# Two-block feed-forward network with 2:4 sparse hidden values on one core: the low part moved to VectorE, and the second down product issued in one piece

## The chip, the core and the metric

The kernel runs on one core of a Trainium2 chip. The metric is the time on the device in microseconds (us); the time before is the median of three runs. The engines are TensorE (PE, with its weight loads as PEld), VectorE (DVE), ScalarE (ACT), GpSimd (POOL) and SyncE (SP), which issues the DMAs.

## The reference

One sequence of 2048 tokens with 256 features passes through six residual parts. The parts are: a feed-forward part with ternary weights, an attention with ALiBi, the same feed-forward part again, a feed-forward part with 2:4 sparse hidden values, an attention with rotary positions, and the sparse part again. Only the sparse part is touched:

```python
def _sparsify_2to4(h):
    g = h.reshape(B, S, I // 4, 4)
    a = jnp.abs(g)
    _, idx = jax.lax.top_k(a, 2)
    mask = (pos == idx[..., 0:1]) | (pos == idx[..., 1:2])
    return (g * mask.astype(g.dtype)).reshape(B, S, I)
h = jax.nn.silu(x @ w_gate) * (x @ w_up)      # x: 2048 x 256, h: 2048 x 1024
return _sparsify_2to4(h) @ w_down             # used as x + 0.5 * f(layernorm(x))
...
```

Of each group of four hidden values the two with the largest magnitude are kept.

## The kernel before

All phases run one after the other on the core. The sparse part is the function ffn_phase with ternary set to false; it runs twice, as ffn1a and as ffn1b. In the profiled execution ffn1a begins at about 860 us and ffn1b at about 1622 us and runs to the end of the kernel.

A phase works through NB = 4 blocks of BLK = 512 tokens. Block 0 and block 3 are written out, blocks 1 and 2 are a hardware loop (blocks_of). The hidden size of 1024 is cut into NCH = 8 chunks of 128, in two halves of GCH = 4 chunks; the host has sorted the weights so that the four members of a sparse group lie in the four chunks of one half at the same place. To keep f32 accuracy each operand of TensorE is a high part plus a low part, and each product is three matmuls (high by high, high by low, low by high).

Each engine has its own program, in order, and semaphores tie them together. For a chunk c of block b:

- TensorE, gate_up(b, c), L361: 12 matmuls of 512 columns into two PSUM banks.
- ScalarE, silu, L431; VectorE, multiply, L485, gives h; ScalarE, side, L451, writes the magnitudes of h into the tile abs.
- VectorE, choose(b, u, i): the 2:4 choice for half u, in four steps. Steps 0 and 1 compare pairs of magnitudes (three operations each, tile win, L502); step 2 adds up ranks (L506 to L509); step 3 finishes them (L512 to L515) and writes the kept values over abs (four operations, L519, semaphore keep).
- ScalarE, hi, L438: the kept values rounded to the high part hh. GpSimd, lo, L580: kept value minus hh gives the low part hl, one 128x512 operation for each chunk, 32 in a phase. A helper lo with the same operation stands in VectorE's program too, but before the change only the ternary phases call it (L490).
- TensorE, down(b, u), L372: 48 matmuls of 256 columns for half u. It waits for all four low parts of the half (semaphore hlo). VectorE, residual, L532, adds the result to the resident x once semaphore dn says that both halves are done.
- For the next block: VectorE's dve_stats at c = 1 and dve_normalise (tile xn, L124) at c = 5, TensorE's transposes(b + 1) (L143) between chunks 6 and 7, ScalarE's act_hi (tile xh, L151) and VectorE's dve_lo (tile xl, L158) at the start of c = 7. Chunk 0 of the next block waits for xl.

The work lags. In the body of block b, VectorE makes the choice of the first half of block b in chunks 4 to 7 and that of the second half of block b - 1 in chunks 0 to 3. TensorE issues down(b - 1, 0) behind chunk 4. It issues down(b - 1, 1) in two pieces: tiles 0 and 1 behind chunk 6, ahead of the transposes, and tiles 2 and 3 behind chunk 7. In block 3 that product is in one piece behind chunk 7. After the last block the rest is drained: choice of the last half, low parts, down(3, 0), down(3, 1), residual. GpSimd does the first four low parts of block b - 1 at the start of its body, then the small power operation rstd for the next layer norm (L136), then the other four.

Of the kernel before, what the change touches and what calls it, by code (L numbers as in the profile page):

```python
# [21 lines left out]
F32 = mybir.dt.float32  # L22
F32R = mybir.dt.float32r
BF16 = mybir.dt.bfloat16
ALU = mybir.AluOpType
# [8 lines left out]
NB = TOK // BLK  # L34
TPB = BLK // P
# [4 lines left out]
NCH = HID // P  # L40
GCH = 4
# [47 lines left out]
def is_first(b):  # L89
    return isinstance(b, int) and b == 0  # L90


def is_last(b):
    return isinstance(b, int) and b == NB - 1
# [204 lines left out]
def ffn_phase(nc, g, name, ternary, out=None, ahead=()):  # L299
# [12 lines left out]
    with ExitStack() as ctx:  # L312
# [32 lines left out]
        @block.tensor  # L345
        def _(e):
            def gate_up(b, c):
                n = b * NCH + c

                if ternary:  # L350
                    if not (is_first(b) and c < 2):
                        e.wait_ge(s.mul, n - 1)
                elif not (is_first(b) and c < 3) and c != 1:
                    e.wait_ge(s.mul, n - 1 if c in (0, NCH - 1) else n - 2)
                for half in range(2):
                    col = half * HID + c * P
                    for k in range(KD):
                        if c == 0 and half == 0:
                            e.wait_ge(s.xlo, b * KD + k + 1)
                        for q, (w, x) in enumerate(terms):  # L360
                            ins = e.matmul(g.ps[:, slots[c] + half, :], w_up[w][:, k, col:col + P], xp[x][:, k, :],  # L361
                                           start=k == 0 and q == 0, stop=k == KD - 1 and q == len(terms) - 1)
                ins.then_inc(s.gu, 1)

            def down(b, u, tiles=range(TPB)):
                e.wait_ge(s.hlo, b * NCH + u * GCH + GCH)
                if u == 0 and not is_first(b):
                    e.wait_ge(s.res, b)
                for j in tiles:
                    todo = [(i, w, x) for i in range(GCH) for w, x in terms]  # L370
                    for q, (i, w, x) in enumerate(todo):
                        ins = e.matmul(g.ps[:, 6 + j // 2, (j % 2) * D:(j % 2 + 1) * D], hp[x][:, u, i, j * P:(j + 1) * P],  # L372
                                       w_dn[w][:, u * GCH + i, :], start=u == 0 and q == 0 and j % 2 == 0,
                                       stop=u == 1 and q == len(todo) - 1, skip_group_check=True)
                if j == TPB - 1:
                    ins.then_inc(s.dn if u else s.dnh, 1)

            def squares(b):

                e.wait_ge(s.sqc, b * NCH + NCH)  # L380
                for j in range(TPB):
                    for u in range(2):
                        ins = e.matmul(g.ps[:, 4, j:j + 1], ssq[:, u, j * P:(j + 1) * P], g.one_col[:, :],
                                       start=j == 0 and u == 0, stop=u == 1, skip_group_check=True)
                ins.then_inc(s.sqs, 1)

            def transposes(b):
                e.wait_ge(s.xn, b + 1)
                if not is_first(b):
                    if ternary and not (isinstance(b, int) and b == 1):  # L390
                        e.wait_ge(s.ms, b - 1)
                    if not ternary:
                        e.wait_ge(s.mul, b * NCH - 3)
                pe_transpose(e, g, s, b, lambda j, k: g.xn[:, j, k * P:(k + 1) * P], TB)

            def body(b):
                for c in range(NCH):
                    gate_up(b, c)
                    if ternary:
                        if c == 2 and not is_first(b):  # L400
                            squares(b - 1)
                            down(b - 1, 1)
                        if c == NCH - 1:
                            down(b, 0)
                    elif not is_first(b):
                        if c == 4:
                            down(b - 1, 0)
                        if c == NCH - 2 and not is_last(b):
                            down(b - 1, 1, range(TPB // 2))
                        if c == NCH - 1:  # L410
                            down(b - 1, 1, range(0 if is_last(b) else TPB // 2, TPB))
                    if c == NCH - 2 and not is_last(b):
                        transposes(b + 1)

            transposes(0)
            blocks_of(e, body)
            if ternary:
                squares(NB - 1)
            else:
                down(NB - 1, 0)  # L420
            down(NB - 1, 1)
# [57 lines left out]
        def _(e):  # L479
# [7 lines left out]

            def lo(b, c):
                e.wait_ge(s.hhi, b * NCH + c + 1)
                e.tensor_tensor(hl[:, c // GCH, c % GCH, :], h32[:, c // GCH, c % GCH, :],  # L490
                                hh[:, c // GCH, c % GCH, :].bitcast(F32), ALU.subtract).then_inc(s.hlo, 1)

            PAIRS = [(0, 1), (0, 2), (0, 3), (1, 2), (1, 3), (2, 3)]
# [32 lines left out]
            def residual(b):  # L526
                if ternary:
                    e.wait_ge(s.inv, b + 1)
                e.wait_ge(s.dn, b + 1)
                for j in range(TPB):  # L530
                    xt = g.x[:, ds(b * TPB + j, 1), :].rearrange("p a d -> p (a d)")
                    ins = e.scalar_tensor_tensor(out=xt, in0=g.ps[:, 6 + j // 2, (j % 2) * D:(j % 2 + 1) * D],  # L532
                                                 scalar=inv[:, j:j + 1] if ternary else 0.5, in1=xt, op0=ALU.mult, op1=ALU.add)
                ins.then_inc(s.res, 1)

            def body(b):
                for c in range(NCH):
                    if c == NCH - 1 and not is_last(b):
                        dve_lo(e, g, s, b + 1, TB)
                    multiply(b, c)  # L540
                    if ternary:
                        if c:
                            lo(b, c - 1)
                        elif not is_first(b):
                            lo(b - 1, NCH - 1)
                        if c == 3 and not is_first(b):
                            mean_squares(b - 1)
                        if c == 6 and not is_first(b):
                            residual(b - 1)
                    elif c >= GCH:  # L550
                        choose(b, 0, c - GCH)
                    elif not is_first(b):
                        choose(b - 1, 1, c)
                    if not is_last(b) and c == 1:
                        dve_stats(e, g, s, b + 1)
                    if not is_last(b) and c == (3 if ternary else 5):
                        dve_normalise(e, g, s, b + 1)
                if not ternary and not is_first(b) and not is_last(b):
                    residual(b - 1)
# [4 lines left out]
            if ternary:  # L564
                lo(NB - 1, NCH - 1)
                mean_squares(NB - 1)
            else:
                for i in range(GCH):
                    choose(NB - 1, 1, i)
                    if i == 1:  # L570
                        residual(NB - 2)
            residual(NB - 1)
            e.wait_ge(s.res, NB)


        @block.gpsimd
        def _(e):
            def lo(b, c):
                e.wait_ge(s.hhi, b * NCH + c + 1)
                e.tensor_tensor(hl[:, c // GCH, c % GCH, :], hs[:, c // GCH, c % GCH, :],  # L580
                                hh[:, c // GCH, c % GCH, :].bitcast(F32), ALU.subtract).then_inc(s.hlo, 1)

            def sum_squares(b, u):
                for i in range(1, GCH):
                    n = b * NCH + u * GCH + i
# [11 lines left out]
                e.tensor_tensor(inv[:, :], ms[:, :], g.mhalf[:, :], ALU.pow).then_inc(s.inv, 1)  # L597

            def body(b):
                if not ternary and not is_first(b):  # L600
                    for c in range(GCH):
                        lo(b - 1, c)
                if not is_last(b):
                    pool_rstd(e, g, s, b + 1)
                if ternary:
                    sum_squares(b, 0)
                    if not is_first(b):
                        inverse(b - 1)
                    sum_squares(b, 1)
                elif not is_first(b):  # L610
                    for c in range(GCH, NCH):
                        lo(b - 1, c)

            pool_rstd(e, g, s, 0)
            blocks_of(e, body)
            if ternary:
                inverse(NB - 1)
            else:
                for i in range(NCH):
                    lo(NB - 1, i)  # L620

        if out is not None:
            @block.sync
# [957 lines left out]
```

## Time and profile before

| | us |
|---|---|
| median of 3 runs (lowest to highest) | 1806.38 (1805.32 to 1822.72) |
| profiled execution, its own time | 1802.62 |
| its span, first to last instruction | 1800.4 |
| busy over the span: PE / DVE / ACT / POOL | 1556.4 / 1283.4 / 950.9 / 306.7 |

The span is 2.2 us shorter than the profiled execution's own time. Busy times of different engines overlap, so they don't add up to the span. The time of an instruction in the timeline runs from its start to its end; one engine's neighbours overlap by about 0.08 us, so that what an instruction adds to a row of others is the distance from start to start.

### The profile page before, as it was taken

The page shows a single profiled execution, that of the slowest core. Times are in us where ns is not written, and L with a number is a line of the kernel's source. Part 1 is how long each engine was busy: PE and PEld are TensorE (multiplying, and loading weights), DVE is VectorE, ACT ScalarE, POOL GpSimd, SP SyncE. Part 2 cuts the span into 40 slices and gives each one's busy share as a digit, 9 for nine tenths or more (in the row PEclk, how much of TensorE's full clock was granted, in tenths as well). Part 3 has the DMA queues.
Part 4 walks back from the last instruction along what each step waited for, and adds up shares of the span by engine and source line. Part 5 has one row for each costly group of instructions (what it writes and reads, how often), then busy time and mean ns, then how long its engine had stood idle before and what let it go on. Part 6 is the DMA issues. An engine that isn't in the chain of part 4 may idle for free. (4 is left out here: it accounts for less than half of the span.)

```text
span 1800.4 us, 33059 instructions
## 1 busy us (share of the span) xinstructions
PE 1556.4 (86%) x13324; PEld 972.3 (54%) x13324; DVE 1283.4 (71%) x1864; ACT 950.9 (53%) x1889; POOL 306.7 (17%) x326
## 2 busy tenths in 40 slices
PE   1598878989999999887799689899999999997996
PEld 0487744444434436676588567444444444366885
DVE  8655647888898832564599786687888988025996
ACT  3345324767777784454334222456686788733342
POOL 5333100000000000232043432000000000030433
PEclk9999869999999999898899888698999999788998
DMA  5000769100000000100100058640000000020000
GB/s 201 24 1 0 127 184 129 34 14 24 13 20 7 2 2 3 46 1 24 35 1 1 1 116 199 87 69 14 20 17 16 11 2 2 2 71 1 12 12 24
DMA packets 37857, 70.54 MB, mean 39 GB/s; under 512 B 5411, under 2 KB 13219, under 8 KB 36645
## 3 DMA queue, kind: packets, MB, share of 16 engines
q1 hardware_dynamic: 37716, 68.58, 16.8%
q8 instruction: 99, 1.62, 0.4%
q14 instruction: 42, 0.34, 0.1%
HBM read 48.90 MB, written 22.15 MB: 39 GB/s over the span
## 5 line engine op out<-in xcount | busy, mean ns | idle before, releaser
L1166 DVE TENSOR_REDUCE l_att_maxima<-psum 128x2 f32<-128x1024 f32 (+3 forms) x640 | 665.0, 1063 | 135.3 <-PE psum L1064 127.6
L1258 ACT ACTIVATE l_att_probs<-psum 128x512 f32<-128x512 f32 (+3 forms) x1280 | 605.6, 531 | 250.3 <-PE psum L1092 227.8
L1109 PE MATMUL psum<-l_att_probs,l_att_v 128*17 128x256 f32 (+2 forms) x4608 | 363.5, 389 | 1.2 <-ACT l_att_o L1265 0.9
L1092 PE MATMUL psum<-l_att_qt,l_kt 51*128 51x512 f32 (+6 forms) x1280 | 331.6, 470 | 7.5 <-ACT l_att_probs L1258 7.5
L1064 PE MATMUL psum<-l_kt,l_att_qt 59*128 59x512 f32 (+7 forms) x1280 | 285.2, 422 | 5.0 <-DVE l_att_maxima L1166 2.6
L1092 PEld LDWEIGHTS psum<-l_att_qt,l_kt 59*128 59x128 f32 (+1 forms) x1280 | 142.6, 194 | 174.0 <-ACT l_att_probs L1258 161.8
L1109 PEld LDWEIGHTS psum<-l_att_probs,l_att_v 128*17 128x17 f32 x4608 | 79.5, 96 | 150.5 <-issue 101.7
L1064 PEld LDWEIGHTS psum<-l_kt,l_att_qt 59*128 59x128 f32 (+1 forms) x1280 | 139.1, 199 | 19.5 <-DVE l_att_maxima L1166 17.4
L1228 POOL CAST l_att_crow<-l_att_cneg 128x16 bf16<-128x16 f32 x32 | 8.1, 252 | 812.6 <-DVE l_att_cneg L1176 812.6
L1061 PE MATMUL psum<-tri 64*128 64x128 bf16 x1024 | 89.1, 237 | 22.0 <-DVE l_att_maxima L1166 18.8
L1090 PEld LDWEIGHTS psum<-tri 64*128 64x128 bf16 x1024 | 33.7, 96 | 101.8 <-ACT l_att_probs L1258 65.6
L1090 PE MATMUL psum<-tri 64*128 64x128 bf16 x1024 | 82.4, 228 | 1.9 <-DMA l_att_qt<-l_att_ct 1.7
L1193 DVE RECIPROCAL l_att_rinv<-psum 128x16 f32<-128x16 f32 x32 | 8.0, 250 | 106.3 <-PE psum L1128 106.3
L1061 PEld LDWEIGHTS psum<-tri 64*128 64x128 bf16 x1024 | 35.8, 101 | 59.8 <-DVE l_att_maxima L1166 34.3
L580 POOL TENSOR_TENSOR ffn1b_hl<-ffn1b_abs,ffn1b_hh 128x512 fp32r<-128x512 f32 x32 | 51.7, 1643 | 84.6 <-ACT ffn1b_hh L438 84.6
L580 POOL TENSOR_TENSOR ffn1a_hl<-ffn1a_abs,ffn1a_hh 128x512 fp32r<-128x512 f32 x32 | 51.7, 1644 | 84.6 <-ACT ffn1a_hh L438 84.6
L136 POOL TENSOR_TENSOR rstd<-var,mhalf 128x4 f32<-128x4 f32 x24 | 24.7, 1027 | 224.8 <-DVE var L115 224.8
L361 PE MATMUL psum<-ffn0b_xh,w_ternary 128*128 128x512 f32 x128 | 53.1, 415 | 9.2 <-DVE ffn0b_h L485 7.8
L361 PE MATMUL psum<-ffn0a_xh,w_ternary 128*128 128x512 f32 x128 | 52.9, 413 | 9.1 <-DVE ffn0a_h L485 7.7
L361 PE MATMUL psum<-ffn1b_xh,wgu_h 128*128 128x512 f32 x128 | 51.5, 402 | 3.9 <-DVE ffn1b_xl L158 2.8
L361 PE MATMUL psum<-ffn1a_xh,wgu_h 128*128 128x512 f32 x128 | 51.3, 400 | 3.9 <-DVE ffn1a_xl L158 2.8
L372 PE MATMUL psum<-wdn_h,ffn1b_hh 128*128 128x256 f32 x128 | 38.8, 303 | 15.6 <-DVE x_resident L532 8.9
(205 smaller groups left out, 2914.5 us busy)
## 6 DMA issues: line engine op xcount, KB each, us to landing
l_kt<-qk_scratch SPq DMA_DIRECT2D x48, 256.0 KB, 10.6
qk_scratch<-l_att_kv_parts SPq DMA_DIRECT2D x22, 512.0 KB, 7.3
l_att_qt<-qk_scratch SPq DMA_DIRECT2D x168, 64.0 KB
qk_scratch<-y SPq DMA_DIRECT2D x10, 512.0 KB, 10.7
set_raw<-in_w_gu SPq DMA_DIRECT2D x2, 1024.0 KB, 6.4
x_resident<-in_x SPq DMA_DIRECT2D x1, 2048.0 KB, 15.4
y<-in_w_gu SPq DMA_DIRECT2D x1, 2048.0 KB, 8.1
raw_down<-in_w_dn SPq DMA_DIRECT2D x2, 1024.0 KB, 8.0
```

The lines of the kernel that those rows point to most:

```text
L136: e.tensor_tensor(g.rstd[:, :], g.var[:, :], g.mhalf[:, :], ALU.pow).then_inc(s.rstd, 1)
L361: ins = e.matmul(g.ps[:, slots[c] + half, :], w_up[w][:, k, col:col + P], xp[x][:, k, :], start=k == 0 and q == 0, stop=k == KD - 1 and q ...
L372: ins = e.matmul(g.ps[:, 6 + j // 2, (j % 2) * D:(j % 2 + 1) * D], hp[x][:, u, i, j * P:(j + 1) * P], w_dn[w][:, u * GCH + i, :], start=u ...
L580: e.tensor_tensor(hl[:, c // GCH, c % GCH, :], hs[:, c // GCH, c % GCH, :], hh[:, c // GCH, c % GCH, :].bitcast(F32), ALU.subtract).then_i ...
L1061: e.matmul(g.ps[:, bank + x, w - P:w], g.tri[half, (2 + m) * P:(3 + m) * P], g.tri[half, m * P:(m + 1) * P], start=m == 0, stop=False, ski ...
L1064: e.matmul(g.ps[:, bank + x, 0:w], qt[rows_of(x), pair, t * P:(t + 1) * P], g.kt[rows_of(x), pair, c * BLK:c * BLK + w], start=c < qb, sto ...
L1090: e.matmul(g.ps[:, i % SB, off:off + P], g.tri[rows, c * P:(c + 1) * P], g.tri[rows, (2 + c) * P:(3 + c) * P], start=c == 0, stop=False, s ...
L1092: e.matmul(g.ps[:, i % SB, off:BLK], g.kt[rows_of(x), hp, kt * P:(kt + 1) * P], qt[rows_of(x), hp, off:BLK], start=u >= TPB, stop=True, sk ...
L1109: ins = e.matmul(g.ps[h * VW:h * VW + HD + 1, OB, lo:hi], g.v[:, kt, STEPS[st][1] * HG + h, :], pr[:, un % PB, h, lo:hi], start=u == 0 and ...
L1166: e.tensor_reduce(mp[:, st % 2, 2 * p:2 * p + 2, t, c], g.ps[:, bank:bank + 2, 0:w], AX.X, ALU.max).then_inc(s.mx, 1)
L1228: e.tensor_copy(cr[:, 0], whole).then_inc(s.cp, 1)
L1258: e.activation(pr[:, un % PB, h, off:BLK], g.ps[:, i % SB, off:BLK], ACT.Exp, scale=HD ** -0.5).then_inc(s.ex, 1)
```

## The change

VectorE now computes the low parts of the sparse phases, GpSimd does not any more. In the body of a block, behind the multiplication of chunk 1 come the low parts of chunks 0 and 1 of the block before, behind that of chunk 2 those of chunks 2 and 3, behind that of chunk 5 those of chunks 4 and 5, and behind that of chunk 6 those of chunks 6 and 7. At the end of the phase the first four stand behind residual(2), and the last four behind the last step of the choice. On TensorE down(b - 1, 1) is issued in one piece behind chunk 7 in every block. The ternary phases keep their instructions.

```diff
-            def down(b, u, tiles=range(TPB)):
+            def down(b, u):
...
                     elif not is_first(b):
                         if c == 4:
                             down(b - 1, 0)
-                        if c == NCH - 2 and not is_last(b):
-                            down(b - 1, 1, range(TPB // 2))
                         if c == NCH - 1:
-                            down(b - 1, 1, range(0 if is_last(b) else TPB // 2, TPB))
+                            down(b - 1, 1)
                     if c == NCH - 2 and not is_last(b):
                         transposes(b + 1)
...
             def lo(b, c):
                 e.wait_ge(s.hhi, b * NCH + c + 1)
-                e.tensor_tensor(hl[:, c // GCH, c % GCH, :], h32[:, c // GCH, c % GCH, :],
+                e.tensor_tensor(hl[:, c // GCH, c % GCH, :], hs[:, c // GCH, c % GCH, :],
...
-                    elif c >= GCH:
-                        choose(b, 0, c - GCH)
-                    elif not is_first(b):
-                        choose(b - 1, 1, c)
+                    else:
+                        if not is_first(b) and c % GCH in (1, 2):
+                            i = c // GCH * GCH + 2 * (c % GCH - 1)
+                            lo(b - 1, i)
+                            lo(b - 1, i + 1)
+                        if c >= GCH:
+                            choose(b, 0, c - GCH)
+                        elif not is_first(b):
+                            choose(b - 1, 1, c)
...
                     if i == 1:
                         residual(NB - 2)
+                        for c in range(GCH):
+                            lo(NB - 1, c)
+                for c in range(GCH, NCH):
+                    lo(NB - 1, c)
             residual(NB - 1)
...
@@ gpsimd @@
-                if not ternary and not is_first(b):
-                    for c in range(GCH):
-                        lo(b - 1, c)
                 if not is_last(b):
                     pool_rstd(e, g, s, b + 1)
...
-                elif not is_first(b):
-                    for c in range(GCH, NCH):
-                        lo(b - 1, c)
...
-            else:
-                for i in range(NCH):
-                    lo(NB - 1, i)
```

## Rows read from the trace of the kernel before

**Rows 1.** Busy time by engine in block 1 of ffn1b; then PEclk, DMA, GB/s

```profile
1663.90:1699.10 35.20, 33.13 (x190) 29.44 (x189) 32.17 (x59) 12.09 (x22) 13.44 (x9) 0.95 0.00 1
```

**Rows 2.** Timeline of PE: start, duration, work, and idle time before with its releaser

```profile
894.56 0.50 PE L361 MATMUL psum<-ffn1a_xh,wgu_h 128*128 128x512 f32 x1 [1.41 <-DVE ffn1a_xl L158]
...
970.65 0.40 PE L361 MATMUL psum<-ffn1a_xh,wgu_h 128*128 128x512 f32 x1
...
1658.37 0.50 PE L361 MATMUL psum<-ffn1b_xh,wgu_h 128*128 128x512 f32 x1 [1.41 <-DVE ffn1b_xl L158]
...
1672.14 0.28 PE L372 MATMUL psum<-wdn_h,ffn1b_hh 128*128 128x256 f32 x1
...
1685.59 0.50 PE L372 MATMUL psum<-wdn_h,ffn1b_hh 128*128 128x256 f32 x1 [2.07 <-POOL ffn1b_hl L580]
...
1727.96 0.32 PE L143 MATMUL psum<-consts,ffn1b_xn 128*128 128x128 f32 x1 [1.20 <-DVE ffn1b_xn L124]
...
1734.53 0.40 PE L361 MATMUL psum<-ffn1b_xh,wgu_h 128*128 128x512 f32 x1
...
1788.17 0.58 PE L372 MATMUL psum<-wdn_h,ffn1b_hh 128*128 128x256 f32 x1 [2.60 <-POOL ffn1b_hl L580]
```

**Rows 3.** Timeline of DVE in block 0 of ffn1b, where GpSimd has no low part

```profile
1649.88 1.89 DVE L502 TENSOR_TENSOR ffn1b_win<-ffn1b_abs 128x512 bf16<-128x512 f32 x3
...
1660.88 2.50 DVE L519 SCALAR_TENSOR_TENSOR ffn1b_abs<-ffn1b_rank,ffn1b_h 128x512 f32<-128x512 bf16 x4
```

**Rows 4.** Timeline of DVE in block 1 of ffn1b, and behind its last block

```profile
1663.30 0.68 DVE L485 TENSOR_TENSOR ffn1b_h<-ffn1b_silu,psum 128x512 f32<-128x512 f32 x1
1663.90 4.60 DVE L502 TENSOR_TENSOR ffn1b_win<-ffn1b_abs 128x512 bf16<-128x512 f32 x3
...
1669.02 2.38 DVE L502 TENSOR_TENSOR ffn1b_win<-ffn1b_abs 128x512 bf16<-128x512 f32 x3
...
1674.02 0.42 DVE L506 TENSOR_TENSOR ffn1b_rank<-ffn1b_win 128x512 bf16<-128x512 bf16 x1
...
1677.42 3.59 DVE L519 SCALAR_TENSOR_TENSOR ffn1b_abs<-ffn1b_rank,ffn1b_h 128x512 f32<-128x512 bf16 x4
...
1681.54 4.55 DVE L502 TENSOR_TENSOR ffn1b_win<-ffn1b_abs 128x512 bf16<-128x512 f32 x3
...
1688.41 1.37 DVE L124 TENSOR_SCALAR ffn1b_xn<-x_resident,mv,rstd 128x256 f32 x4
...
1739.57 0.68 DVE L485 TENSOR_TENSOR ffn1b_h<-ffn1b_silu,psum 128x512 f32<-128x512 f32 x1
...
1769.87 6.89 DVE L502 TENSOR_TENSOR ffn1b_win<-ffn1b_abs 128x512 bf16<-128x512 f32 x6
...
1780.92 3.61 DVE L519 SCALAR_TENSOR_TENSOR ffn1b_abs<-ffn1b_rank,ffn1b_h 128x512 f32<-128x512 bf16 x4
1795.68 1.42 DVE L532 SCALAR_TENSOR_TENSOR x_resident<-psum,x_resident 128x256 f32<-128x256 f32 x4 [11.15 <-PE psum L372]
```

**Rows 5.** Timeline of POOL: the low parts of half a block

```profile
1678.85 6.68 POOL L580 TENSOR_TENSOR ffn1b_hl<-ffn1b_abs,ffn1b_hh 128x512 fp32r<-128x512 f32 x4 [4.37 <-ACT ffn1b_hh L438]
```

**Rows 6.** One tile's instructions, ffn0a_hl: a low part on VectorE, min/median/max ns

```profile
L490 DVE TENSOR_TENSOR ffn0a_hl<-ffn0a_h,ffn0a_hh x32: 679/684/1768, 73.8 to 174.3; 128x512 fp32r<-128x512 f32 x32
```

**Rows 7.** Timeline of ACT at the start of block 2 of ffn1b

```profile
1699.58 0.60 ACT L431 ACTIVATE ffn1b_silu<-psum 128x512 f32<-128x512 f32 x1 [3.53 <-PE psum L361]
...
1702.68 0.59 ACT L431 ACTIVATE ffn1b_silu<-psum 128x512 f32<-128x512 f32 x1
```

**Rows 8.** Stretches behind gaps of PE, columns as in the first group

```profile
802.05:804.05 2.00, 2.00 (x6) 1.52 (x5) 0.75 (x2) 0.13 (x1) 0.00 (x0) 0.50 0.00 0
...
1686.00:1687.00 1.00, 1.00 (x7) 1.00 (x7) 1.00 (x3) 0.21 (x1) 0.00 (x0) 0.50 0.00 0
1724.00:1725.00 1.00, 1.00 (x11) 1.00 (x10) 1.00 (x3) 0.17 (x1) 0.00 (x0) 1.00 0.00 0
```

**Rows 9.** Timeline of DVE: the last residual of ffn1a

```profile
1030.37 0.76 DVE L532 SCALAR_TENSOR_TENSOR x_resident<-psum,x_resident 128x256 f32<-128x256 f32 x2 [9.72 <-PE psum L372]
```

More of the change, by code:

```diff
@@ L368, in down @@
                     e.wait_ge(s.res, b)
-                for j in tiles:
+                for j in range(TPB):
                     todo = [(i, w, x) for i in range(GCH) for w, x in terms]
@@ L374, in down @@
                                        stop=u == 1 and q == len(todo) - 1, skip_group_check=True)
-                if j == TPB - 1:
-                    ins.then_inc(s.dn if u else s.dnh, 1)
+                ins.then_inc(s.dn if u else s.dnh, 1)
             def squares(b):
@@ L577, in _ @@
         def _(e):
[L578 to L581, printed above, removed]
             def sum_squares(b, u):
```

## The prediction

> **What bounds the kernel now.** I read the groups of instructions first: everything that the diff touches lies in ffn1a and ffn1b, the rest keeps its instructions, so only these two phases can move. Then the busy time by stage, for block 1 of ffn1b: TensorE is busy 33.1 of 35.2 us and VectorE 32.2 [rows 1]. Neither is idle enough to ignore, so what matters is which waits for which. The timelines tell. From the first matmul of block 1 to that of block 3 pass 76.2 us in ffn1b and 76.1 in ffn1a, so 38.1 for a block [rows 2]. What TensorE needs without waiting is a good deal less: five products of chunks plus 0.17 us for the start take 1672.14 - 1658.37 = 13.77 us, so a chunk is 2.72 us, eight are 21.8, and 96 down matmuls of 0.12 us are 11.5; with the transposes (0.85 us to the next start) that makes 34.2 us. The missing 4 us in each block are two waits: 2.07 us for the low parts of GpSimd ahead of the first piece of down(b - 1, 1), and 1.20 us for xn ahead of the transposes, or in block 1 of ffn1b a lower clock in the place of the second [rows 2, 8]. Both are VectorE's doing in the end. It is never idle in these blocks but for some 2.8 us ahead of xl, and part of its work is stretched. Three comparisons take 1.89 us in block 0, where GpSimd has no low part to do, and 4.60 and 4.55 us in block 1 where GpSimd has; four kept values take 2.50 against 3.59 us [rows 3, 4]. GpSimd's four low parts run 6.68 us beside them [rows 5].
>
> **What the change removes.** The low parts leave GpSimd, so the stretches should go. From the first multiplication of block 1 to the end of xn, VectorE loses (4.60 - 1.89) + (2.38 - 1.89) + (3.59 - 2.50) + (4.55 - 1.89) = 7.0 us to them [rows 3, 4]. Behind the last block six comparisons take 6.89 us where 3.6 would do, and four kept values 3.61 against 2.50 [rows 4]. The 2.07 us wait for GpSimd goes as well.
>
> **What it adds on VectorE.** One low part of the same shape and types takes 0.684 us in the ternary phase, so 0.60 us from start to start [rows 6]; the upper end, 1.77 us in the same row, belongs to the overlap with GpSimd and does not come here, since GpSimd keeps only its 1 us power operation in a block. Eight a block are 4.8 us. Six of them stand ahead of xn: 3.6 us against the 7.0 saved.
>
> **What it moves on TensorE.** The first 24 matmuls of down(b - 1, 1) (2.9 us) move from ahead of the transposes to behind chunk 7. They used to fill time in which xn was not ready. Now they follow xn, in a row with everything else. The question is therefore what xn waits for.
>
> **A middle block step by step.** From start to start an operation adds some 0.08 us less than its duration: a multiplication or comparison 0.60, a rank 0.34 and four 1.34, four kept values 2.42, the normalisation 1.29, the residual 1.33; the statistics add 2.1, from the comparisons' end at 1671.3 to the multiplication ahead of 1674.02 [rows 3, 4]. Take the first matmul of the block as 0. Chunks 0 to 4 end at 2.7, 5.5, 8.2, 10.9 and 13.6. ScalarE starts silu 0.28 us behind chunk 0 and VectorE multiplies 0.63 us later, at 3.6, if it is free. Comparisons to 6.0. The second silu starts 3.1 us behind the first, since four roundings to hh stand ahead of it [rows 7], so the second multiplication starts at 6.7. Then two low parts to 8.5, comparisons to 10.3, statistics (2.1) to 12.4, multiplication to 13.0, two low parts to 14.2. down(b - 1, 0) may start at 14.3, 0.7 us late, and ends at 20.0; chunk 5 ends at 22.8. VectorE meanwhile does ranks to 15.5, multiplication 16.1, ranks 17.6, kept values 20.0, multiplication 20.6, comparisons 22.4, and then waits for chunk 5: its multiplication starts only at 23.7. Behind it stand two low parts (25.5), comparisons (27.3) and the normalisation, to 28.6. TensorE has finished chunk 6 at 25.5 and is idle for 3.2 us. Transposes to 29.6, chunk 7 to 32.4, the whole second down product to 38.2. VectorE has xl, the last choice and the residual (1.33 us) done by 40.3, ahead of the next multiplication at 38.2 + 3.6, so it delays nothing; ScalarE's magnitudes now wait for low parts a little longer, but each is done before the next silu can start. So the period is 38.2 us, against 38.1. What was saved on VectorE is spent on its own added work, on the wait for chunk 5 (which sits behind down(b - 1, 0)) and on the 2.9 us that now follow xn.
>
> **Block 1** starts with VectorE late, its first multiplication at 4.9 (1663.30 - 1658.37) [rows 2, 4], as now. By the same steps down(0, 0) starts at 15.0, xn ends at 29.2 and the block lasts 38.8 us. The two blocks together: 77.0 against 76.1, 0.9 us worse in each phase.
>
> **The last block and the drain** have no xn. VectorE's first multiplication starts at 3.6 and not at 1739.57 - 1734.53 = 5.0 [rows 2, 4]. Multiplication 5 starts at 23.0, behind chunk 5; two low parts, comparisons, multiplication, two low parts, ranks, multiplication and the choice bring VectorE to 34.2, the six comparisons to 37.8, the residual to 39.1, four low parts to 41.5. down(3, 0) runs from 41.7, at the lower clock at its start, as it does now, to 48.8. VectorE's ranks and kept values end at 46.7 and its last low part at 49.3, since the last rounding to hh must come first. So down(3, 1) starts at 49.4, right behind down(3, 0), 5.8 us at the full clock, and the last residual starts at 55.4. Now it starts at 1795.68 - 1734.53 = 61.2 in ffn1b and 1030.37 - 970.65 = 59.7 in ffn1a [rows 2, 4, 9]. That is 5.8 and 4.3 us gained; some 1.5 us of ffn1b's share is the lower clock behind the 2.60 us gap at 1788.17, which goes with the gap.
>
> Sum without the clock: 2 x 0.9 - 5.8 - 4.3 = -8.3 us.
>
> **The clock.** The new gap of some 3.2 us ahead of the transposes comes four times in the two phases. Of the eleven gaps of 2.07 to 2.60 us that the trace has in the feed-forward phases, five were followed by the lower of the two levels (0.50 is 1.2 GHz, 1.00 is 2.4 GHz), as at 1686 and 802 us, and six were not, as at 1724 us [rows 8]. One such stretch cost 1.6 us: the 24 matmuls from 1685.59 us took 4.47 us to the next start, where 24 x 0.12 = 2.88 would do [rows 2]. Everything behind the gap is in a row, so this price is paid in full. For a longer gap I take three falls in four, +4.8 us; the ends are none (0) and all four (+6.4).
>
> The Trainium skill, page "TensorE: Matmul & The Clock Gate", section "Part 1: The HAM clock gate", says that the check of activity runs free of the kernel, so that the same kernel can meet a fall in one execution and miss it in the next. By it the sum would be anything between -8.3 and -1.9 us, without a preference for three. The trace agrees in kind: two gaps of the same 2.07 us ended differently.
>
> Total: -8.3 + 4.8 = -3.5 us. The profiled execution, 1802.62 us, lies 3.8 us under the median of the runs, 1806.38. I apply the sum to the median: **1802.9 us**, 0.2% faster. A measurement of this kernel tells about 1%, 18 us, from no change.
>
> **Rivals.**
>
> *No or one fall of the clock.* The same walk, -8.3 to -6.7 us: 1798 to 1800 us. Six of eleven gaps speak for it, their being shorter against it.
>
> *TensorE never waits.* If xn were ready when chunk 6 ends, the period would be 34.2 us: four periods by 3.8 us and the drain's 10.1 give -25 us, 1781 us. For it speaks that VectorE's own work without stretches is only some 33 us a block. Against it: the multiplication behind chunk 5 and the 4.9 us between it and the end of xn lie in a row, and xn would have to come 3.1 us sooner than I find.
>
> *The stretches stay (the slower side).* If the comparisons and kept values are long for another reason than GpSimd (reads of ScalarE and writes to the same tile, say), the added 0.60 us come on top. First multiplication to end of xn is 26.5 us now [rows 4]; with 3.6 more, and 3.6 ahead and 9.6 behind it (start of transposes, 0.1; transposes and chunk 7, 3.7; down, 5.8), the period is 43.3 us, 5.3 more, four times. In the drain the last kept value, 45.0 us behind the first multiplication now [rows 4], moves by 12 x 0.6 = 7.2, and the last down product starts at about 58.3 where it is 53.6 now [rows 2]: 4.7 us, twice. Together +30 us, 1836 us, 1.7% slower. It decides from the point where less than half of the 7.0 us goes. Against it stands that none of the three comparisons or kept values of block 0 is stretched, and every stretched stretch has a low part of GpSimd beside it [rows 3 to 5].
>
> The Trainium skill, page "SBUF — State Buffer", section "SBUF: two separate sides", describes a port pair that VectorE and GpSimd hold in turn for a whole instruction, when VectorE reads two inputs from SBUF. By it the stretches end with GpSimd's low parts and this rival is worth little; the multiplications, which read one input from PSUM, keep 0.68 us beside GpSimd, which agrees [rows 4].
>
> **Chances.** Forecast (two to four falls) 0.64, no or one fall 0.25, TensorE never waits 0.04, the stretches stay 0.03, and 0.04 for runs of the whole kernel that scatter beyond 1% on either side. The walk with none to four falls gives 1798.1 to 1804.5; the drain's second product at the lower clock in both phases adds 3; a low part at its full 0.68 in place of 0.60 us adds 0.5 in each of four blocks, 2 in all; a gap shorter by 1 us in each takes 4 off. That makes 1794 to 1809. Faster by over 1%: 0.06; within 1%: 0.90; slower by over 1%: 0.04.
>
> **What would show it.** Right: comparisons of 1.89 us in all blocks; down(b - 1, 1) as 48 matmuls behind chunk 7; a gap of TensorE of about 3 us ahead of the transposes, released by xn; VectorE idle for about 1 us ahead of the multiplication of chunk 5; periods near 38 us, or 39.8 with a lower clock; no gap above 1 us ahead of the last down product. Wrong: a gap ahead of the transposes under 1 us, comparisons still above 2 us, or VectorE busy until the next block's first multiplication.

## The result and the profile after

| | us |
|---|---|
| before, 20 runs: median (lowest to highest), mean | 1804.76 (1788.81 to 1827.86), 1807.5 |
| changed, 20 runs: median (lowest to highest), mean | 1812.20 (1798.03 to 1818.45), 1810.1 |
| ratio, changed to before | 1.0051, 95% interval 1.0029 to 1.0073 |
| profiled execution of the changed kernel, its span | 1818.45, 1816.3 |

I forecast 1802.9 us, 0.2% faster, in a range of 1794 to 1809. The median came out at 1812.2, 0.5% slower by the ratio. That ratio leaves out runs that lie over 1.5% above the fastest of their own kernel; five of before (1817 to 1828 us) fall under this and none of the changed one, although the means of all runs are only 2.6 us apart. With all 20 runs of each, the ratio is 1.0014 by the means and 1.0041 by the medians, and the difference of the means, 2.6 us, has a 95% interval of 5.2 us to either side (worked out from the spread of the runs). So these two sets alone do not show that the changed kernel is slower.

So where did the time go? First the touched phases. I take each from its first transpose to its last residual. In the first trace of before ffn1a took 1030.37 - 863.28 = 167.1 us and ffn1b 1795.68 - 1626.37 = 169.3. In the changed kernel ffn1a takes 1035.46 - 867.90 = 167.6 and ffn1b 1811.60 - 1644.53 = 167.1. Together they are 1.8 us shorter, 334.6 against 336.4. The profiled execution as a whole is 15.8 us longer, so all of that and 1.8 us more lie in stages that the change does not touch: 13 us in the second attention, the rest in the stages ahead of ffn1a.

TensorE in ffn1b after the change, timeline of single instructions (start, duration, work, idle time before and its releaser); the counterparts are [rows 2]:

```profile
1676.53 0.50 PE L361 MATMUL psum<-ffn1b_xh,wgu_h 128*128 128x512 f32 x1 [1.41 <-DVE ffn1b_xl L158]
...
1706.15 0.32 PE L143 MATMUL psum<-consts,ffn1b_xn 128*128 128x128 f32 x1 [3.17 <-DVE ffn1b_xn L124]
...
1717.15 0.40 PE L361 MATMUL psum<-ffn1b_xh,wgu_h 128*128 128x512 f32 x1
...
1731.64 0.38 PE L372 MATMUL psum<-wdn_h,ffn1b_hh 128*128 128x256 f32 x1 [0.70 <-DVE ffn1b_hl L487]
...
1746.29 0.98 PE L143 MATMUL psum<-consts,ffn1b_xn 128*128 128x128 f32 x7 [3.17 <-DVE ffn1b_xn L124]
...
1755.75 0.40 PE L361 MATMUL psum<-ffn1b_xh,wgu_h 128*128 128x512 f32 x1
...
1797.42 0.58 PE L372 MATMUL psum<-wdn_h,ffn1b_hh 128*128 128x256 f32 x1 [7.14 <-DVE ffn1b_hl L487]
```

Read the brackets: the wait for GpSimd is gone, and a wait of 3.17 us for xn stands ahead of the transposes, where there was 1.20 [rows 2]. The blocks begin at 1676.53, 1717.15 and 1755.75, so they last 40.6 and 38.6 us, 79.2 together, where it was 76.2.

VectorE in block 2, from its first multiplication to xn, and the last residuals of both phases; the counterparts are [rows 3, 4, 9]:

```profile
1035.46 1.42 DVE L529 SCALAR_TENSOR_TENSOR x_resident<-psum,x_resident 128x256 f32<-128x256 f32 x4 [6.10 <-PE psum L372]
...
1720.90 0.69 DVE L482 TENSOR_TENSOR ffn1b_h<-ffn1b_silu,psum 128x512 f32<-128x512 f32 x1 [1.49 <-ACT ffn1b_silu L428]
1721.50 1.89 DVE L499 TENSOR_TENSOR ffn1b_win<-ffn1b_abs 128x512 bf16<-128x512 f32 x3
1723.98 0.69 DVE L482 TENSOR_TENSOR ffn1b_h<-ffn1b_silu,psum 128x512 f32<-128x512 f32 x1 [0.59 <-ACT ffn1b_silu L428]
1724.59 1.29 DVE L487 TENSOR_TENSOR ffn1b_hl<-ffn1b_abs,ffn1b_hh 128x512 fp32r<-128x512 f32 x2
...
1734.90 2.50 DVE L516 SCALAR_TENSOR_TENSOR ffn1b_abs<-ffn1b_rank,ffn1b_h 128x512 f32<-128x512 bf16 x4
...
1741.16 0.69 DVE L482 TENSOR_TENSOR ffn1b_h<-ffn1b_silu,psum 128x512 f32<-128x512 f32 x1 [1.35 <-ACT ffn1b_silu L428]
1741.76 1.29 DVE L487 TENSOR_TENSOR ffn1b_hl<-ffn1b_abs,ffn1b_hh 128x512 fp32r<-128x512 f32 x2
1742.97 1.89 DVE L499 TENSOR_TENSOR ffn1b_win<-ffn1b_abs 128x512 bf16<-128x512 f32 x3
1744.78 1.38 DVE L124 TENSOR_SCALAR ffn1b_xn<-x_resident,mv,rstd 128x256 f32 x4
...
1811.60 1.42 DVE L529 SCALAR_TENSOR_TENSOR x_resident<-psum,x_resident 128x256 f32<-128x256 f32 x4 [6.48 <-PE psum L372]
```

The stretches are gone: 1.89 and 2.50 us where it was 4.55 and 3.59. No single comparison of the two phases takes more than 0.69 us. The low parts cost 1.29 us for two. VectorE, which had no idle time at this place before, now waits 1.35 us ahead of the multiplication of chunk 5 (1741.16), and everything from there to xn is in a row. The multiplication came at 24.0 us of the block (1741.16 - 1717.15), the walk had 23.7; the transposes at 29.1, the walk had 28.7.

The clock behind two of the gaps, as busy time of each engine in a stretch, with PEclk third from the right:

```profile
1706.99:1708.00 1.01, 1.01 (x6) 0.87 (x5) 1.01 (x3) 0.00 (x0) 0.00 (x0) 0.65 0.00 0
...
1748.00:1749.00 1.00, 1.00 (x6) 0.82 (x5) 1.00 (x4) 0.00 (x0) 0.00 (x0) 1.00 0.00 0
```

After the same gap of 3.17 us the clock fell in block 1, 0.3 us into the first stretch (so that the mean of the stretch is 0.65), and not in block 2. In ffn1a of the same trace it fell in both blocks. That is three falls in four.

### The profile page after: what moved, and what is told of

Its sections match the earlier page's. It is cut to its first block and busy times, and to the rows that moved or that the text cites. A ratio compares the mean times of both kernels' runs of the same rounds, so it can differ in the third digit from the quotient of the medians.

```text
span 1816.3 us, 33055 instructions
## 1 busy us (share of the span) xinstructions
PE 1573.4 (87%) x13324; PEld 978.0 (54%) x13324; DVE 1271.5 (70%) x1928; ACT 951.3 (52%) x1889; POOL 203.7 (11%) x262
## 5 line engine op out<-in xcount | busy, mean ns | idle before, releaser
L1101 PE MATMUL psum<-l_att_probs,l_att_v 128*17 128x256 f32 (+2 forms) x4608 | 368.1, 393 | 1.2 <-ACT l_att_o L1257 0.9
L1084 PE MATMUL psum<-l_att_qt,l_kt 51*128 51x512 f32 (+6 forms) x1280 | 335.5, 477 | 7.5 <-ACT l_att_probs L1250 7.5
L1056 PE MATMUL psum<-l_kt,l_att_qt 59*128 59x512 f32 (+7 forms) x1280 | 290.7, 431 | 5.0 <-DVE l_att_maxima L1158 2.2
L361 PE MATMUL psum<-ffn0a_xl,w_ternary 128*128 128x512 f32 x128 | 52.4, 410 | 0.0
L361 PE MATMUL psum<-ffn0b_xl,w_ternary 128*128 128x512 f32 x128 | 52.3, 408 | 0.0
L361 PE MATMUL psum<-ffn1a_xl,wgu_h 128*128 128x512 f32 x128 | 51.5, 403 | 0.0
```

The costliest lines, as they stand in the source:

```text
L1056: e.matmul(g.ps[:, bank + x, 0:w], qt[rows_of(x), pair, t * P:(t + 1) * P], g.kt[rows_of(x), pair, c * BLK:c * BLK + w], start=c < qb, sto ...
L1084: e.matmul(g.ps[:, i % SB, off:BLK], g.kt[rows_of(x), hp, kt * P:(kt + 1) * P], qt[rows_of(x), hp, off:BLK], start=u >= TPB, stop=True, sk ...
L1101: ins = e.matmul(g.ps[h * VW:h * VW + HD + 1, OB, lo:hi], g.v[:, kt, STEPS[st][1] * HG + h, :], pr[:, un % PB, h, lo:hi], start=u == 0 and ...
```

## The experiments

**The kernels against themselves.** The first question is whether the 0.5% is the change's. I ran each kernel again, three times, with no edit.

> The kernel before, unchanged, timed against itself. Theory 1 (the touched phases moved by about -2 us as the walk had it, and the 0.5% came from scatter of TensorE's clock in stages that the change doesn't touch): ratio within 0.996 to 1.004 of 1, with single runs from 1795 to 1825 us in both; ffn1b from its first transpose to its last residual again 169 to 170 us, ffn1a 167 to 168. Rival (the change makes the untouched stages slower, by its placement in memory or by the moment at which they start): the ratio is 1 too, but the spread of single runs is too small to make 7 us between two medians of 20.

> The changed kernel again, unchanged. Theory 1: the two touched phases take 167 to 168.5 us each as in its first trace, and the ratio comes out anywhere from 0.997 to 1.005, since it hangs on the clock in the attention stages. Rival: the ratio is 1.004 to 1.006 again, and the attention stages again take some 10 us more than in the trace of the kernel before.

> The kernel before once more against itself. Theory 1 (scatter of the clock in untouched stages): mean of all runs 1804 to 1808 us, ratio 0.996 to 1.004. Rival (the 7 us between the first two medians are the change's): this kernel's mean lies 5 us or more under that of the changed kernel on the same chip.

> The changed kernel once more, beside the kernel before on the same chip. Theory 1: touched phases 167 to 168.5 us each, mean of all runs within 4 us of that of the kernel before, on either side. Rival: 5 to 9 us over it.

> The kernel before against itself, a third time. Theory 1: ratio anywhere from 0.994 to 1.004; the second attention stage, from the last residual of ffn1a to the first transpose of ffn1b, takes 589 to 609 us with a mean clock of 0.92 to 0.88. Rival (long attention stages of 604 us and more belong to kernels with the low parts on VectorE): 589 to 597 us, and mean of all runs 3 us or more under the changed kernel beside it.

> The changed kernel a third time. Theory 1: mean of all runs within 4 us of the kernel before beside it, on either side; phases 167 to 168 us. Rival: 3 to 9 us over it, attention stage 604 us or more.

The ratio of each job compares with further runs of the kernel before in that job, the reference runs. The first two of these six runs were in one job, the next two in a second and the last two in a third, each on another chip.

| run | ratio to before, 95% | mean of its 12 runs | ffn1a, ffn1b |
|---|---|---|---|
| aa_before (before itself) | 1.0035, 0.9988 to 1.0081 | 1807.7 | 167.1, 169.5 |
| after_again (changed) | 1.0042, 0.9999 to 1.0085 | 1807.5 | 167.8, 167.2 |
| aa_before2 (before itself) | 0.9942, 0.9903 to 0.9981 | 1806.1 | 169.9, 169.3 |
| after_again2 (changed) | 0.9945, 0.9903 to 0.9987 | 1804.4 | 167.9, 167.1 |
| aa_before3 (before itself) | 0.9976, 0.9927 to 1.0026 | 1805.2 | 170.1, 170.0 |
| after_again3 (changed) | 1.0004, 0.9969 to 1.0038 | 1801.6 | 167.6, 167.2 |

The kernel before differs from itself by +0.35% in one job and by -0.58% in the next, there with an interval that excludes 1 and below the 0.996 that I had expected. Beside it the changed kernel lies 0.2, 1.7 and 3.6 us lower by the mean. Over the three jobs, 36 runs each, that is 1804.5 against 1806.4 us, a difference of -1.9 us with a 95% interval of about 4.7 us to either side (worked out from the spread of the single runs, 8.3 and 11.6 us). The reference runs say the same with more scatter. The changed kernel's mean is 3.3 us over theirs in the first job and 7.5 and 5.6 us under theirs in the other two, and with them the kernel before has a mean of 1807.0 us in 116 runs (one of 1935 us, at a clock of 0.73, left out), so that the changed kernel is 2.5 us lower, with an interval of 3.3 us to either side. My 4 us to either side thus hold against the repeated runs and not against the reference runs, and single runs of the kernel before go from 1786 to 1826 us, further than I had. The ratio of after_again, 1.0042, lies in the range of theory 1 and in that of its rival and decides nothing. But the rival's 5 to 9 us slower are out, and theory 1 holds. The touched phases can be read much more finely. Both together take 334.6, 335.0, 334.9 and 334.8 us in the four traces of the changed kernel, and 336.4, 336.6, 339.2 and 340.1 in the four of before: by their means 3.2 us less.

Where does the scatter lie? I took the stage from the last residual of ffn1a to the first transpose of ffn1b, the second attention, which is the same code in both. Busy time by engine, PEclk third from the right. First the kernel before in its first trace (each line is a view of its own kernel):

```profile
1030.37:1626.37 596.00, 549.05 (x5312) 280.71 (x5313) 422.44 (x531) 351.20 (x723) 59.29 (x92) 0.90 0.23 47
```

the changed kernel in its first trace:

```profile
1035.46:1644.50 609.04, 561.89 (x5312) 284.33 (x5312) 422.44 (x531) 351.46 (x723) 59.40 (x92) 0.88 0.22 46
```

the kernel before again, in its first, second and third repeat:

```profile
1032.21:1621.20 588.99, 541.52 (x5313) 279.97 (x5313) 422.50 (x531) 350.11 (x723) 59.25 (x92) 0.92 0.23 48
```

```profile
1036.28:1645.70 609.42, 562.33 (x5312) 285.88 (x5312) 422.64 (x531) 351.52 (x723) 59.26 (x92) 0.88 0.23 46
```

```profile
1035.92:1627.20 591.28, 543.85 (x5313) 281.00 (x5313) 422.46 (x531) 350.56 (x723) 59.24 (x92) 0.91 0.23 48
```

and the changed kernel again, first and second repeat:

```profile
1038.08:1628.93 590.85, 543.92 (x5312) 281.11 (x5313) 422.40 (x531) 350.25 (x723) 59.28 (x92) 0.91 0.23 48
```

```profile
1031.85:1636.50 604.65, 558.15 (x5313) 283.44 (x5313) 422.58 (x531) 351.20 (x723) 59.28 (x92) 0.89 0.23 47
```

The second column is the length: 589 to 609 us for the same work, long where PEclk is 0.88 or 0.89 and short where it is 0.90 to 0.92. VectorE is busy 422.4 to 422.6 us in all seven. TensorE's idle time in the stage, the second column less the third, is 46.5 to 47.5 us in all seven too: only its busy time grows, from 541.5 to 562.3 us. So longer waits are not what makes the stage long. Each kernel is found at both ends, the kernel before at 589.0 and 609.4 us and the changed one at 590.9 and 609.0. So this one stage scatters by 20 us with the clock, several times what the change moved, and it does so without the change. Over all traces of this study it took over 600 us in four of the eight with the low parts on VectorE, and in one of the six with them on GpSimd (aa_before2). That is too few to say whether the long case is as frequent in both; if it were much more frequent the means above would show it, and they don't.

The record has the mean granted clock of whole executions as well, for 133 runs of the kernel before (the one of 1935 us left out) and for all 56 of the changed one. The time follows it closely (correlation -0.98): 0.01 less of the clock goes with 14 us more. With this line taken off, the changed kernel is 1.9 us shorter than the kernel before at the same clock, with a 95% interval of 0.7 us to either side. This is an estimate from a straight line through all runs. The first 20 runs of the changed kernel had a mean clock of 0.924 and its later 36 had 0.9275, which by the line is 5 of the 5.6 us between their means.

**lo_only.** Low parts on VectorE, down product in two pieces as before:

```diff
+                        if c == NCH - 2 and not is_last(b):
+                            down(b - 1, 1, range(TPB // 2))
                         if c == NCH - 1:
-                            down(b - 1, 1)
+                            down(b - 1, 1, range(0 if is_last(b) else TPB // 2, TPB))
```

> Low parts on VectorE as in the change, but down(b - 1, 1) in two pieces as before. Walk: the first piece waits for the low part of chunk 7, which stands behind the multiplication of chunk 6 on VectorE, to 30.5 us; period 39.9 us, with the lower clock behind a gap of 5 us 41.5 us, against 39.8 in the changed kernel; ffn1b about 170.5 us, ratio to before 1.001 to 1.007. Rival (issuing in one piece is what costs, since its 2.9 us follow xn): period under 38 us, ffn1b under 165 us, ratio under 0.998.

Ratio 1.0083 (1.0043 to 1.0123), ffn1a and ffn1b 172.7 and 172.6 us. TensorE's timeline, the first matmul of the first piece:

```profile
1707.30 0.58 PE L372 MATMUL psum<-wdn_h,ffn1b_hh 128*128 128x256 f32 x1 [4.88 <-DVE ffn1b_hl L490]
```

The first piece waits 4.88 us for the low part of chunk 7, as the walk had it. The blocks last 42.1 and 43.2 us where I had 41.5, the phase is 2 us longer than my number, and the ratio lies above my range. The rival falls.

**down_only.** The other half: one piece behind chunk 7, low parts still on GpSimd.

```diff
-                        if c == NCH - 2 and not is_last(b):
-                            down(b - 1, 1, range(TPB // 2))
                         if c == NCH - 1:
-                            down(b - 1, 1, range(0 if is_last(b) else TPB // 2, TPB))
+                            down(b - 1, 1)
```

> The kernel before with down(b - 1, 1) in one piece behind chunk 7, low parts still on GpSimd. Walk: VectorE stays stretched, so xn ends 26.5 us behind the first multiplication and nothing fills the wait; gap ahead of the transposes about 5 us, period 39.8 us plus 1.6 for the clock; the 2.07 us wait for GpSimd goes. ffn1b and ffn1a about 172 to 174 us each against 169.3 and 167.1, ratio 1.003 to 1.007. Rival (one piece is free or better, the wait for GpSimd was the cost): period 36 to 38 us, both phases under 168 us.

Ratio 1.0111 (1.0009 to 1.0212, four runs), both phases 177.4 us. VectorE's timeline keeps the stretched comparisons:

```profile
1688.37 4.54 DVE L499 TENSOR_TENSOR ffn1b_win<-ffn1b_abs 128x512 bf16<-128x512 f32 x3
...
1695.23 1.37 DVE L124 TENSOR_SCALAR ffn1b_xn<-x_resident,mv,rstd 128x256 f32 x4
```

and TensorE's shows the gap ahead of the transposes:

```profile
1696.74 0.47 PE L143 MATMUL psum<-consts,ffn1b_xn 128*128 128x128 f32 x1 [6.41 <-DVE ffn1b_xn L124]
```

The direction was right and the size too small, 177.4 where I had 172 to 174, and the ratio is above my range. The gap is 6.4 us in block 1 and 6.0 in block 2, not 5, and behind the second of these gaps the transposes and chunk 7 took 6.4 us in place of 3.6, so a fall of the clock can cost 2.7 us and not only 1.6. Over both phases low parts alone cost 8.9 us against the first trace of before (345.3 - 336.4), one piece alone 18.4, and both together save 1.8. The first piece can't start early when the low parts wait in VectorE's row, and xn is too late for one piece as long as VectorE is stretched, so each half pays only with the other one.

**early.** The changed kernel with xn ahead of the wait for chunk 5, and so also ahead of the multiplication, two low parts and three comparisons that stand behind that wait:

```diff
-                    if not is_last(b) and c == (3 if ternary else 5):
+                    if not is_last(b) and c == (3 if ternary else 4):
                         dve_normalise(e, g, s, b + 1)
```

> The changed kernel with the normalisation of the next block at chunk 4 in place of chunk 5, ahead of the wait for chunk 5. Theory of the walk (xn behind the late chunk 5 makes TensorE wait 3.2 us in each middle block, and the gap costs 1.6 us of lower clock): xn is ready at 23.7 us, ahead of chunk 6's end at 25.5, no gap ahead of the transposes, period 35.0 us against 39.8; 9.6 us less in each phase, ffn1b about 157.5 us, ratio to before about 0.989 to 0.991. Rival (VectorE as a whole is the bound and gets late elsewhere): the gap moves ahead of chunk 0 or of xl, period above 37 us, ratio above 0.996.

Ratio 0.9919 (0.9882 to 0.9957), mean 1785.8 us beside 1807.5 for the changed kernel in the same job. ffn1a and ffn1b take 157.1 us each where I had 157.5, together 20.4 us less than in the changed kernel's first trace. The ratio is just above my range. TensorE's timeline in ffn1b:

```profile
1671.96 1.03 PE L143 MATMUL psum<-consts,ffn1b_xn 128*128 128x128 f32 x8
...
1681.55 0.40 PE L361 MATMUL psum<-ffn1b_xh,wgu_h 128*128 128x512 f32 x1
...
1696.03 0.39 PE L372 MATMUL psum<-wdn_h,ffn1b_hh 128*128 128x256 f32 x1 [0.69 <-DVE ffn1b_hl L487]
...
1716.97 0.40 PE L361 MATMUL psum<-ffn1b_xh,wgu_h 128*128 128x512 f32 x1
```

The transposes have no bracket any more, and block 2 lasts 35.4 us. The place of xn, behind the wait for chunk 5 and the work that follows it, was the new bound of the changed kernel: this shows it directly.

**before_early.** The same one-line edit in the kernel before.

> The kernel before with the normalisation at chunk 4. Walk: xn is ready ahead of the end of the first piece of the down product, so only the 1.2 us waits for xn go: ffn1a 164.7 us against 167.1, ffn1b about 168 against 169.3, ratio 0.996 to 1.000. Rival (the place of the normalisation is worth as much here as in the changed kernel): 10 us less in each phase, ratio 0.99.

Ratio 1.0015 (0.9974 to 1.0055), a little above my 1.000. ffn1a took 166.8 us and ffn1b 164.4, together 5.2 us less than in the first trace of before (6.9 less than the mean of its four traces), where I had 3.7; the split is off, since the clock fell in both middle blocks of ffn1a here and in none of ffn1b. The period of ffn1b's block 2 without a fall is 36.5 us. So the early xn is worth 5 to 7 us in the kernel before and 20 in the changed one, and it is the change that makes it worth having.

**early_c5.** In addition down(b - 1, 0) behind chunk 5:

```diff
-                        if c == 4:
+                        if c == 5:
                             down(b - 1, 0)
```

> The changed kernel with the normalisation at chunk 4 and down(b - 1, 0) behind chunk 5 in place of chunk 4. Walk: the 0.7 us wait (1.1 in block 1) for the low part of chunk 3 goes, and so does VectorE's wait for chunk 5; period 34.3 us, TensorE's own work, against 35.0; in the last block chunk 6 and no longer chunk 5 sets VectorE's time, 0.9 us earlier. Each phase 2.7 us under that of early (157.1), so 154.4, ratio to before 0.987 to 0.991. Rival (VectorE is now the bound at 35 us): no change against early.

Ratio 0.984 (0.9762 to 0.9919), mean of six runs 1777.5 us; ffn1a 156.0, ffn1b 155.6, so 2.5 us less than early together where I had 5.4. It ran on another chip than early. The repeat took 155.4 and 155.6 us:

> The fastest version again: both phases 155.5 to 156.5 us, mean of all runs 20 to 27 us under the kernel before, ratio 0.985 to 0.989.

Its ratio is 0.9806 (0.9731 to 0.9882), under the range that I had, and its mean 1783.3 us; all twelve runs have a mean of 1780.4 us. TensorE's timeline in the first of the two shows why so little came of it:

```profile
1680.23 0.39 PE L372 MATMUL psum<-wdn_h,ffn1b_hh 128*128 128x256 f32 x1 [0.99 <-DVE ffn1b_hl L487]
...
1715.47 0.39 PE L372 MATMUL psum<-wdn_h,ffn1b_hh 128*128 128x256 f32 x1 [0.78 <-DVE ffn1b_hl L487]
```

The wait moved: now the second down product waits 0.8 to 1.0 us for VectorE's last low part. The rival is half right, VectorE begins to be the bound. By its phases this is the fastest version, 25 us less than the first trace of before over both phases (336.4 - 311.6) and 1.3 to 1.5% by the means (1777.5 against 1804.9 us of the kernel before in the first of its two jobs, 1783.3 against 1807.2 in the second); against early alone the intervals of the whole time overlap.

## Why the prediction was wrong

*The stretches go with GpSimd's low parts.* Right: 1.89 and 2.50 us in all blocks, and 4.54 again in down_only, where GpSimd keeps them. The slower rival (*the stretches stay*) is out.

*The cost of a low part.* Right: 1.29 us for two, 0.60 from start to start.

*The middle block.* Right in its mechanism, step by step; 38.6 us where I had 38.2, block 1 40.6 with a fall where 38.8 + 1.6 was forecast. *TensorE never waits* is out, but early shows that it was one line away.

*The clock.* Three falls in four in the first trace, as taken; the other three traces of the same kernel have two, two and three. So the three of the first trace were partly luck. The falls are not spread evenly: ffn1b's block 1 fell and its block 2 held in all four traces, ffn1a's block 2 fell in all four, and only its block 1 changed, with 40.7 us in two traces and 39.1 in the other two. The difference is the 1.6 us that I had taken. The Trainium skill, page "TensorE: Matmul & The Clock Gate", section "Part 1: The HAM clock gate", says that the window in which the chip watches TensorE's activity is free-running, so that the number of matmuls at the lower clock differs from run to run of the same kernel. In kind ffn1a's block 1 agrees; why three of the four places came out alike each time stays open.

*The last block and the drain.* Right: the last down product follows the one before it and the last residual starts 1811.60 - 1755.75 = 55.9 us into the block, where I had 55.4.

*The sum for the phases.* -3.5 us forecast; -1.8 in the first pair of traces and -3.2 by the means of four and four. In the first trace ffn1b's middle blocks are 0.2 and 0.4 us and its last block with the drain 0.5 us longer than the walk, and ffn1a's 0.3, 0.3 and 0.1. That is the whole difference between -3.5 and -1.8.

*The total.* This is the step that failed: "I apply the sum to the median". The sum was put on a median of three runs, and the range of 1794 to 1809 was made of terms of the two touched phases alone. The scatter of everything else was put at nothing. The prediction even says that 18 us can't be told from no change, and gave 0.04 to scatter beyond 1%, but scatter below 1% had no term in the range, and it was enough: the median of the changed kernel came out 3 us beyond its end, with the touched phases where the walk had them. The median moves by more than the change, without any change: the kernel before's 20 runs here and its reference runs in the later jobs (17 to 35 each) have medians from 1804.8 to 1813.3 us. One untouched stage took 591 to 609 us in the changed kernel alone and 589 to 609 in the kernel before, with the clock that was granted, and the kernel before differs from itself by 0.35% and 0.58%. I had the sign of this in the three runs that I was shown, 1805 to 1823 us. The ratio of 1.0051 is of that size, and in the three later jobs the changed kernel lies beside the kernel before or slightly under it. That the first 20 runs lay higher by 7.4 us in the median is therefore not shown to be the change's; what sets the clock in the attention of a given execution stays open.

## What to carry to other kernels

When work is moved to an engine to free another, ask what then stands in a row: here the saved stretches (7.0 us a block) were lost again, half to the low parts that now stand ahead of xn (3.6 us), the rest because the next block's layer norm stood behind a wait that had not mattered before, with work behind xn that had stood ahead of it. Moving that one step ahead of the wait gave 20 us, several times the change itself. Two edits can each cost time alone and be free together, so test them together too.

And before a fraction of a per cent is explained, time the kernel against itself; if it is not at 1, compare the touched stages in the traces, where a few tenths of a us can be read.

## What was not expected of the hardware

- TensorE's mean granted clock over one attention stage was 0.88 to 0.92 from one execution to the next, with 20 us between the shortest and the longest of one kernel (589.0 and 609.4 us), on the same instructions and with the same idle time.
- A fall of the clock cost 1.6 us behind gaps of 2.07 us (1685.59 us of the kernel before) and of 3.17 us (ffn1a's block 1 with and without it), and 2.7 us behind one of 6.0 us in down_only.
- After identical gaps of 3.17 us the clock fell in ten blocks of sixteen (four traces of the changed kernel) and held in six, in three of the four places the same way each time.
